# First batch of an attention and expert kernel: first group's operands loaded alone, low parts on VectorE, two score units a tile

## The reference, cut to what matters

```python
xn = _layernorm(x)                                   # x: (8, 512, 128)
# attention
q, k, v = split(xn @ w_in.T + b_in)                  # 16 heads, hsz = 8
scores = einsum('bhqd,bhkd->bhqk', q * hsz**-0.5, k) + causal_bias
attn = softmax(scores)
a = nan_to_zero(einsum('bhqk,bhkd->bhqd', attn, v) @ w_out.T + b_out)
# experts: E = 8, top 2, F = 176; the shared one has 352 columns
s = softmax(xn @ gate_w.T)
topk_w, topk_i = top_k(s, 2)
combine = scatter(topk_i, topk_w / (topk_w.sum(-1) + 1e-20) * 2.5)
g = silu(einsum('td,edf->etf', xn, w_gate)) * einsum('td,edf->etf', xn, w_up)
y = einsum('te,etd->td', combine, einsum('etf,efd->etd', g, w_down))
y = y + (silu(xn @ sw_gate) * (xn @ sw_up)) @ sw_down
return x + a + y
```

## Time and profile before

| What | us |
|---|---|
| Median of 3 executions (590.12 to 592.05) | 590.14 |
| The profiled execution, its own time | 590.31 |
| Its span, first to last instruction | 588.6 |
| From the start to the first exponential of batch 0's attention | 81.77 |
| TensorE, VectorE, ScalarE, GpSimd busy over the span | 532.2, 473.4, 342.3, 331.5 |

### The profile page before, as it was taken

The page is one execution under the profiler, slowest core; times in us unless marked ns, Lnnn a source line. Parts: engine busy times, 40 slices in busy tenths (PEclk is TensorE's granted clock), DMA queues, the critical chain, the costliest instruction groups (busy, mean ns, idle before and its releaser), DMA issues.

```text
span 588.6 us, 13213 instructions
## 1 busy us (share of the span) xinstructions
PE 532.2 (90%) x4568; PEld 299.6 (51%) x4568; DVE 473.4 (80%) x831; ACT 342.3 (58%) x463; POOL 331.5 (56%) x350
## 2 busy tenths in 40 slices
PE   2667899998999999999999999999999999999985
PEld 2334552565426663366525763366625764266622
DVE  5997878899777988689787988689886998679804
ACT  5412279453893459634794359734695348843593
POOL 2265545576355764478355783468454783548642
PEclk9878999998999999999999999999999999999999
DMA  9885005900269003850069003760058202690001
GB/s 268 253 204 126 2 30 176 249 8 1 64 179 234 2 11 129 210 126 0 18 183 253 19 9 107 193 165 0 9 179 220 65 0 77 176 225 1 11 1 36
DMA packets 45629, 62.03 MB, mean 105 GB/s; under 512 B 4800, under 2 KB 29984, under 8 KB 45600
## 3 DMA queue, kind: packets, MB, share of 16 engines
q1 hardware_dynamic: 42892, 58.40, 37.1%
q10 hardware_dynamic: 2708, 3.24, 1.7%
HBM read 45.24 MB, written 15.34 MB: 103 GB/s over the span
## 4 chain that ended last, share of the span: by engine, by line
PE 61%; DVE 13%; ACT 10%; issue 8%; POOL 4%; DMA 3%; SPq 0%; POOLq 0%; DVEq 0%; ACTq 0%
PE banks L631 9%; ACT probs L866 7%; PE banks L494 7%; PE banks L529 7%; PE banks L496 6%; PE banks L495 6%; PE banks L510 6%; PE banks L604 6%; DVE neg_max L1194 5%; PE banks L511 3%; PE banks L512 3%; POOL hid_lo L954 2%; DVE probs L1169 1%; PE banks L520 1%; POOL probs L948 1%
## 5 line engine op out<-in xcount | busy, mean ns | idle before, releaser
L1194 DVE TENSOR_REDUCE neg_max<-banks 128x2 f32<-128x1024 f32 (+3 forms) x224 | 194.8, 915 | 24.3 <-PE banks L520 23.3
L866 ACT ACTIVATE probs<-banks 128x1024 f32<-128x1024 f32 x160 | 155.4, 1031 | 11.4 <-PE banks L604 9.0
L976 POOL TENSOR_SCALAR_AFFINE_SELECT probs<-probs 128x512 f32<-128x512 f32 x128 | 91.4, 736 | 122.1 <-ACT probs L866 122.1
L803 ACT ACTIVATE probs<-banks 128x512 f32<-128x512 f32 (+1 forms) x112 | 66.9, 597 | 146.0 <-PE banks L496 145.3
L954 POOL TENSOR_TENSOR hid_lo<-probs,hid_hi 128x512 fp32r<-128x512 f32 (+1 forms) x88 | 115.7, 1316 | 61.9 <-ACT hid_hi L810 61.9
L948 POOL TENSOR_TENSOR probs<-probs,cb 128x512 f32<-128x512 f32 x88 | 112.9, 1283 | 63.6 <-ACT probs L803 63.6
L494 PE MATMUL banks<-x_hi,w_hi 128*128 128x512 f32 (+1 forms) x224 | 95.2, 425 | 5.5 <-DVE probs L1169 5.5
L631 PE MATMUL banks<-probs,v_op 128*32 128x512 f32 (+3 forms) x1024 | 95.2, 444 | 3.7 <-POOL probs L976 3.5
L1169 DVE TENSOR_TENSOR probs<-probs,banks 128x512 f32<-128x512 f32 (+1 forms) x112 | 76.0, 680 | 21.8 <-POOL probs L948 15.5
L496 PE MATMUL banks<-x_hi,w_lo 128*128 128x512 f32 (+1 forms) x224 | 89.9, 401 | 0.0
L495 PE MATMUL banks<-x_lo,w_hi 128*128 128x512 f32 (+1 forms) x224 | 89.7, 400 | 0.0
(11 more groups left out here) (136 smaller groups left out, 565.5 us busy)
## 6 DMA issues: line engine op xcount, KB each, us to landing
q_op<-q_dram SPq DMA_DIRECT2D x16, 512.0 KB, 6.4
k_op<-k_dram SPq DMA_DIRECT2D x16, 512.0 KB, 7.6
cb<-c_dram SPq DMA_DIRECT2D x31, 256.0 KB, 4.5
cb<-c_dram SPq DMA_DIRECT2D x16, 224.0 KB, 4.7
q_dram<-q_parts SPq DMA_DIRECT2D x8, 384.0 KB, 2.5
k_dram<-k_parts SPq DMA_DIRECT2D x8, 384.0 KB, 2.6
cb<-c_dram SPq DMA_DIRECT2D x16, 192.0 KB, 4.5
cb<-c_dram SPq DMA_DIRECT2D x15, 160.0 KB, 4.4
```

The costliest lines, as they stand in the source:

```text
L866: nc.scalar.activation(probs[:, g % 2, 2 * u:2 * u + 2, :], ring[:, at:at + 2, :], ACT.Exp).then_inc(exp_done, 1)
L976: return nc.gpsimd.affine_select(out=view, in_=view, compare_op=ALU.is_ge, fill=0.0, base=0, pattern=[[0, 4], [1, P]], channel_multiplier=-1)
L1194: return nc.vector.tensor_reduce(out, in_, AX.X, ALU.max, negate=True)
```

## The change

It touches batch 0 only. SyncE sends each part of q and k as soon as it is split, k's smallest DMA first, and loads the operands of the first group (256 KB of q, 256 KB of k, semaphore `ops_first`), then those of the second, then as before. TensorE takes two units at each of the tiles 3 to 12, one ahead of `gate_up` and one behind it. VectorE makes the constants before the splits, `low_hidden` of tiles 0 to 2 and `low_down`; GpSimd no longer makes these. `normalise(1)` and the maxima's transpose come after the last unit, at tile 12 and 13, and ScalarE's copies of both after its table load; `place_v` moves from tile 2 to tile 6.

```diff
-PAIRS_FIRST = [3 * int(4 <= k <= 9) + 2 * int(k == 10) for k in range(NT + 2)]
+MAXIMA_AT_FIRST = NT - 1
+UNITS_FIRST = [2 * int(3 <= k <= 12) for k in range(NT + 2)]
+LO_FIRST = NT - ROUTED
...
+            def first_parts_out():
...
+                q_out(1, 0, 3, 0)
+                q_out(3, 3, 2, 1)
+                q_out(4, 5, 1, 2)
+                k_out(1, 5, 1)
+                k_out(3, 3, 2)
+                k_out(4, 0, 3)
+
+            def first_operands_in():
+                sp.wait_ge(slots_written, 2 * 16)
+                sp.wait_ge(q_written, PART_WRITES * 16)
+                for g, loaded in ((0, ops_first), (1, ops_loaded[0])):
+                    own = slice(g * PAIRS // GROUPS, (g + 1) * PAIRS // GROUPS)
+                    for op, dram in ((q_op, q_dram), (k_op, k_dram)):
+                        if g == 0 and op is k_op:
+                            sp.wait_ge(k_written, PART_WRITES * 16)
+                        sp.dma_start(op[:, own, :].rearrange("p i n -> p (i n)"),
+                                     dram[:, :, :, own, :].rearrange("t s d i n -> (s d) t (i n)")
+                                     ).then_inc(loaded, 16)
...
-            q_parts_out(0)
-            k_parts_out(0)
-            sp.wait_ge(slots_written, 2 * 16)
-            operands_in(0, None, 0)
+            first_parts_out()
+            first_operands_in()
...
+            def first_experts_and_maxima():
...
+                for k in range(NT + 2):
+                    if k == 1:
+                        transpose_comb(0)
+                    units = UNITS_FIRST[k]
+                    if units:
+                        pair(0, None, n)
+                    if k < NT:
+                        gate_up(0, k)
+                    if units >= 2:
+                        pair(0, None, n + 1)
...
+                    if k == MAXIMA_AT_FIRST:
+                        transpose_maxima(0)
+                    if k >= 2:
+                        down(0, k - 2, None)
...
+                    if k == MAXIMA_AT_FIRST:
+                        transpose_x(1)
+                    n += units
...
                     if k == NT - 1:
 
                         nc.scalar.activation(table_call[:, :], bqk[:, 1:2], ACT.Exp)
...
+                    if k == NT - 1 and i is None:
+                        take_maxima(b)
+                        take_xT(b + 1)
...
+                if isinstance(b, int) and b == 0 and k == LO_FIRST:
+                    pool.wait_ge(hid_lo_done, LO_FIRST)
...
-                    if 1 <= k <= NT - LATE:
+                    if (LO_FIRST + 1 if i is None else 1) <= k <= NT - LATE:
                         low_hidden(b, k - 1)
-                    if k == 2:
-                        if i is None:
-                            low_down()
+                    if k == (6 if i is None else 2):
                         place_v(b, i)
...
+            def first_experts_and_maxima():
+
+                hidden(0, 0)
+                hidden(0, 1)
+                low_routed(0)
+                low_hidden(0, 0)
+                low_routed(1)
+                hidden(0, 2)
+                low_hidden(0, 1)
+                low_hidden(0, 2)
+                low_down()
+                n = 0
+                for k in range(LO_FIRST, NT + 1):
+                    units = UNITS_FIRST[k]
+                    if units:
+                        pair(0, None, n)
+                    if k > LO_FIRST:
+                        hidden(0, k - 1)
+                    for m in range(1, units):
+                        pair(0, None, n + m)
+                    n += units
+                    if units and n == NAT_ALL:
+                        split_maxima(0)
+                        normalise(1)
...
             router_weights(0)
+            constants()
             take_combT(0)
```

More of the change, by code:

```diff
@@ L684, in pair @@
                 scores(b, i, n // NAT_PAIRS, n % NAT_PAIRS)
+            def first_experts_and_maxima():
[10 more added lines that the diff above has]
+                        pair(0, None, n + 1)
+                    if k == NT:
+                        project_k(1)
+                        project_v_and_logits(1, vl)
+                        scores_t(0, 0, 0)
+                    if k == NT + 1:
+                        scores_t(0, 0, 1)
+                    if k == MAXIMA_AT_FIRST:
+                        transpose_maxima(0)
+                    if k >= 2:
+                        down(0, k - 2, None)
+                    if units >= 3:
+                        pair(0, None, n + 2)
+                    if k == MAXIMA_AT_FIRST:
+                        transpose_x(1)
+                    n += units
             def experts_and_maxima(b, i, front):
-                pairs_at = PAIRS_FIRST if i is None else PAIRS_AT
-                n = 0 if i is None else EARLY
+                n = EARLY
                 for k in range(NT + 2):
-                    if k == 1 and i is None:
-                        transpose_comb(0)
-                    if k < NT and (k >= 2 or i is None):
+                    if 2 <= k < NT:
                         gate_up(b, k)
-                    if k == 2 and i is not None:
+                    if k == 2:
                         transpose_o(i, 1)
-                    ahead = int(k < EARLY and i is not None)
-                    late = int(2 <= k < 4 and i is not None)
-                    for _ in range(pairs_at[k] - ahead - late):
+                    ahead = int(k < EARLY)
+                    late = int(2 <= k < 4)
+                    for _ in range(PAIRS_AT[k] - ahead - late):
                         pair(b, i, n)
@@ L712, in experts_and_maxima @@
                         down(b, k - 2, i)
-                    if k == 2 and i is not None:
+                    if k == 2:
                         transpose_on(i)
-                    if k == 3 and i is not None:
+                    if k == 3:
                         project_out(i)
@@ L839, in experts @@
                         high_routed_down()
-                    if 1 <= k < NT - LATE_HIGH:
+                    if 1 <= k < NT - LATE_HIGH or (i is None and k == NT - 2):
                         high_hidden(b, k - 1)
@@ L990, in attend @@
                          ).then_inc(masked, 1)
-            def low_down():
-                pool.wait_ge(routed_lo, 2)
-                pool.wait_ge(wd_hi_done, 3)
-                for tiles in (slice(0, HALF_WD), slice(HALF_WD, ROUTED)):
-                    nc.gpsimd.tensor_tensor(wd_lo[:, tiles, :], wd_raw[:, tiles, :], wd_hi[:, tiles, :].bitcast(F32),
-                                            ALU.subtract).then_inc(wd_lo_done, 1)
             experts(0, None)
@@ L1324, in experts_and_maxima @@
                         normalise(b + 1)
-                    if k == 2 and i is not None:
+                    if k == 2:
                         normalise_o(i, 1)
-                    for m in range(pairs_at[k]):
-                        if k == 1 and m == 1 and i is not None:
+                    for m in range(PAIRS_AT[k]):
+                        if k == 1 and m == 1:
                             take_o(i, 1)
-                        if k == 3 and m == 1 and i is not None:
+                        if k == 3 and m == 1:
                             add_attention(i)
@@ L1384, in low_shared, with low_down @@
                                             wd_hi[rows, tiles, :].bitcast(F32), ALU.subtract).then_inc(shared_lo, 1)
+            def low_down():
+                dve.wait_ge(wd_hi_done, 3)
+                for tiles in (slice(0, HALF_WD), slice(HALF_WD, ROUTED)):
+                    nc.vector.tensor_tensor(wd_lo[:, tiles, :], wd_raw[:, tiles, :], wd_hi[:, tiles, :].bitcast(F32),
+                                            ALU.subtract).then_inc(wd_lo_done, 1)
             def low_routed(w):
```

50 lines of the change are left out of this document (32 added, 18 removed).

## The result

The changed kernel takes 595.42 us (median of 14 executions, 592.70 to 596.68), the kernel before 590.05 (14 executions, 589.16 to 592.05). The ratio is 1.0082, with a 95% interval from 1.0065 to 1.0098: slower by 0.8%, as forecast in sign, 1.7 us above the forecast of 593.7 and inside its range. The profiled execution itself took 593.91, with a span of 592.2; it is one of the quicker ones.

A forecast was written before the change was run, and what follows sets the result against it. No engine fills batch 0's opening; waits set its length. Upper clock +0.1, two lower-clock spells +2.2 and +1.4, later low-part waits -0.2: +3.5 us on the profiled 590.31, written as 593.7, range 586.8 to 596.5.

The forecast's parts named there:

- early spell: TensorE's clock halves after the wait for the first maximum, between about 38.5 and 41.8 us: costs 2.2 us (1.5 to 2.9).
- late spell: TensorE's clock halves after the near-empty stretch at the end of the stage, before the first exponential: costs 1.4 us.
- Parts out: SyncE's queue: writes of q and k parts past at 30.1 us, against 31.6 before; casts ahead of the splits cost 0.25.
- operands in: Load of the first group: its k half takes 3.5 us, so operands are there at 33.6, 5.4 us sooner.
- The chain: From operands landing through silu of tile 3, tile 2's high part, `low_hidden`, `low_down`: 7.0 us, first maximum at 40.6.
- The tiles: Tiles 4 to 12: TensorE paces them at 3.3 to 3.35 us each, VectorE needing 3.1; nine take 30.1 us.
- rival two: Faster: operands at 32.0, `low_hidden` not behind the weighing, VectorE's 3.1 pacing tiles; 586.6 us, chance 0.17.
- The end: From tile 13 to batch 0's first exponential: 9.9 to 10.0 us, including 1.8 for the normalisation now on the path.
- The wash: Opening at the upper clock: earlier operands offset by chain, extra tiles and end; first exponential 81.9 against 81.77, +0.1 us.
- The clock: Two stretches with TensorE idle in batch 0's opening halve its clock: 2.2 plus 1.4, together 3.6 us.
- rival one: The clock does not fall, or falls once: 590.2 to 592.0 us, chance 0.27.
- rival three: Splitting the load brings little: first group lands near 36.0, everything 2.4 us later; 596.1 us, chance 0.14.

The follow-up runs named there:

- e1: Changed kernel plus 23 idle matmuls that nobody reads, filling both TensorE gaps (before unit 2 and around the maxima's transpose): 589.86 us, ratio 0.9983 to the kernel before.
- e2: Changed kernel with one ScalarE operation moved: the high part of tile 2 ahead of the silu of tile 3; 589.93 us, ratio 0.9988 to the kernel before.
- e8: Changed kernel with `low_down` back on GpSimd, ahead of its first weighing; 591.26 us, ratio 1.0016 to the kernel before.
- e9: e4 with both score units behind gate and up from tile 4 on, and `hidden` ahead of both maxima; 582.86 us, ratio 0.9864 to the kernel before.
- e3: Changed kernel with batch 1 normalised before `low_hidden` of tile 2, and x transposed right behind the maxima, ahead of down of tile 11; 588.83 us, ratio 0.9975.
- e6: Changed kernel with the parts' order and the single first 1 MB load of the kernel before; 599.37 us, ratio 1.0148 to the kernel before.
- e5: Changed kernel with idle matmuls only in the late gap, around the transpose of the maxima; 591.40 us, ratio 1.0022 to the kernel before.
- e4: Changed kernel with the edits of both e2 and e3; 584.61 us, ratio 0.9896 to the kernel before.

## Why the prediction was right, and where it was not

The sign, the place and the course were right. Against the profiled execution of the changed kernel, step by step:

| Step | forecast | measured |
|---|---|---|
| queue past the parts' writes | 30.1 | 30.55 |
| k half of the first group | 3.5 | 4.08 |
| operands there | 33.6 | 34.63 |
| operands to first maximum | 7.0 | 6.6 |
| first maximum | 40.6 | 41.23 |
| tile 4's unit | 41.8 | 42.58 |
| a tile at the upper clock | 3.3 to 3.35 | 3.33 |
| gate of tile 13, spell in it | 74.1 | 73.96 |
| from there to the first exponential, without a spell | 10.0 | 9.4 |
| clock, early spell (gate of tile 13 against e1's, 72.48) | 2.2 | 1.5 |
| clock, late spell (first exponential against e1's, less the early one) | 1.4 | 2.2 |
| first exponential | 85.5 | 85.59 |
| rest of the kernel | -0.2 | -0.2 |
| this execution | 593.8 | 593.91 |

That the last lines fit to 0.1 us is luck. Tile 4 came 0.8 later than forecast, the early spell cost 0.7 less, the nine tiles took 0.2 less, the end without its spell 0.6 less, and the late spell cost 0.8 more; these cancel.

**Parts out and operands in.** Both were taken too short, 1.0 us together. The last part write took 5.80 us, where the 4.9 of the earlier trace rows was used; the load took 4.08, near its upper bound of 4.3, where 3.5 was taken from halving the time of 512 KB. Here a DMA of half the size did not take half the time. The three casts ahead of the splits, put at 0.25, cost 0.04 (the k split starts at 22.37 instead of 22.33), since VectorE had been idle there; and the row that the 0.25 is said to come from, four such operations in 1.12 us, would have given three of them 0.84.

**The chain.** The theory held link by link: gate to silu 1.69 (35.44 to 37.13) as forecast, silu start to the end of the weighing 2.0 (37.13 to 39.15) as forecast, `low_down` 1.60 as forecast. One link was put wrongly: `low_hidden` doesn't start behind the weighing, it is issued at 38.27 and stands in it, and is done 0.55 after the weighing, not 0.8. That it was held is shown by its length, 1.43 beside the weighing and 0.68 without. By this the rule of the Trainium skill named in the prediction ("SBUF — State Buffer", Who interferes with whom) agrees with this trace. e2 shows that the chain was the wait, and e8 that `low_down` was its last link.

**The tiles.** TensorE paces them at 3.33, and not VectorE at 3.1: rival two fell. The sum's 0.15 for one more change between kinds of matmul has no row behind it; e9, where the two units stand together and `hidden` ahead of both maxima, needs 0.35 less a tile than the changed kernel.

**The end.** The path was as forecast, 9.4 without the spell (11.6 minus 2.2) against 10.0. The normalisation took 1.2 to the next operation instead of 1.8, and it was the estimate between 1.12 and 4.28 that was too high.

**The wash.** At the upper clock the change was to be worth +0.1, less 0.2 later. e1 is the nearest to that case: its first exponential is at 81.94 against 81.77, +0.2, and its time is 1.0 us under the kernel before by the ratio (0.2 to 1.8 by the interval). Right in kind, and too high by 0.9. It isn't quite a comparison at one clock, since the 81.77 of the kernel before holds that kernel's own spell of 6.8 us. What filling its gaps would give was not tried, so what the change is worth with neither kernel at the lower clock stays open.

**The clock.** This is the term that was mis-sized. 3.6 us were forecast, 2.2 for the early spell and 1.4 for the late one; over all executions they cost 5.8, 2.3 and 3.5. The early one agrees with 2.3 by the ratios, whose interval is wide; in the profiled executions it cost 1.5, which is what the prediction's own rate gives for the 3.4 us that it lasted (0.43 each). For the late one 1.4 was taken where the prediction itself said that 3.2 us of work on the path could double, "as the fall may come late". It came early enough: both projections, the values' and the first scores are at 1.2 GHz in the rows above, 2.2 us in the profiled execution, and more on average. How much longer it lasts in the slower of the 14 executions is not seen, since one of them was profiled; their mean granted clock is 0.971 to 0.977, against 0.978 to 0.983 in the five quickest.

With 5.8 in place of 3.6 and the wash at -1.0 the sum would have been 590.1 + 4.8 = 594.9; this only restates the ratio of 1.0082, since both terms come from e1. With both spells gone the changed kernel is 1.0 us under the kernel before, and with them 4.8 over it, so they turned the sign. They were not the only thing that could: with them in part, moving one operation brought the kernel level with the one before (e2, -0.7, an interval that takes in no change), and the two moves of e3 brought it under (-1.5).

One more stretch at the lower clock stands in both the changed kernel and e1: from 34 to 39 us the clock is at 0.50, behind the wait for the operands, and gate to silu of tile 3 takes 1.69 us where the kernel before, at 1.00, took 0.99 (35.20 to 36.19). The prediction had this in its chain; what filling that wait would give was not tried.

The prediction weighed the page "TensorE: Matmul & The Clock Gate" (Part 1) of the Trainium skill, which puts the ramp penalty under 1% of a typical kernel. The two spells here, behind gaps in the middle of the kernel, cost 1.0% by e1, 0.6% in the profiled executions. So pricing them as a term was right.

**The rivals.** One (the clock does not fall) is what e1 makes: its forecast of 590.2 against 589.86. Two needed the operands at 32.0 and a tile of 3.1, and neither came. Three is refuted by e6, and by the operands at 34.63 where it put them near 36.0. In the chances, a third of 0.42 with rival one's 0.27 is 0.41 and not 0.39, and the rest with rival three is 0.42 and not 0.44; nothing hangs on it.

## What to carry to other kernels

When a load is made earlier, walk every engine's order from the moment it lands: the gain here was 4 us, and a single instruction on ScalarE that stood behind a later tile's work, one place out of order, took more than all of it, the clock behind its gap included (e2 gave back 5.5). When an edit leaves TensorE a gap before work on the critical path, such as the 2.6 us and the 3.4 us here, price the lower clock behind the gap as a term of its own, and test it by filling the gap with matmuls that nobody reads. An operation that is free under a wait (the normalisation here) must be moved together with the cover: once the wait is shorter, put it under the next one.

## What the runs showed of the hardware that was not expected

- Idle matmuls paid more than was expected. e1 issues 23 matmuls more than the changed kernel and is 1.0% faster, with the clock at 1.00 through both gaps.
- A shorter gap can save the clock altogether. Ahead of unit 2 TensorE was idle for 2.61 us in the changed kernel, 2.58 in e5 and 2.04 in e3, and each time its clock fell to 1.2 GHz; it was idle for 1.13 in e8 and the clock stayed. At the end of the stage it fell in e9 behind 1.94 us and stayed in e4 behind 1.08. The length of one gap doesn't settle it, though: in the kernel before it fell at 40.7 in a wait of 1.16 us that began 0.7 us behind the end of one of 2.31.
- The second spell of the kernel before, at 139.7 us in batch 1, doesn't appear in the profiled execution of the changed kernel, though the order there is the same: the clock is 1.00 in each microsecond from 142 to 152. In e1 it is 0.62 and 0.53 over 138 to 142. So a spell outside the changed part can come or go between executions, and one profile of each kernel doesn't tell a change from it.
- VectorE's 512-column subtraction beside GpSimd took 1.41 to 1.43 us beside a weighing of 1.27, and 2.03 beside the two `wd_lo` operations of 4.12 in e8, against 0.68 alone.
